# Attention: masked score tiles spread among the whole ones, where two followed each other at the end of a query tile

## What is computed

```python
q, k, v = split_heads(x @ Wq.T), split_heads(x @ Wk.T), split_heads(x @ Wv.T)
sim = einsum('bhid,bhjd->bhij', q, k) / sqrt(hd)
sim = where(causal_mask, neg, sim)
exp_sim = exp(sim - max(sim, axis=-1))
denom = sum(exp_sim, axis=-1) + exp(denom_bias)      # attention a; b has no bias
out = einsum('bhij,bhjd->bhid', exp_sim / denom, v)
```

## Time and profile before

| | us |
|---|---|
| median of 3 runs | 5185.71 (5184.31 to 5189.25) |
| the profiled execution | 5181.14 |
| its span | 5179.4 |
| PE busy | 4608.4 (89%) |
| DVE busy | 4098.5 (79%) |
| ACT busy | 3144.7 (61%) |
| POOL busy | 1188.4 (23%) |

### The profile page before, as it was taken

The page is one execution under the profiler, slowest core; times in us unless marked ns, Lnnn a source line. Parts: engine busy times, 40 slices in busy tenths (PEclk is TensorE's granted clock), DMA queues, the critical chain, the costliest instruction groups (busy, mean ns, idle before and its releaser), DMA issues. The chain is left out here.

```text
span 5179.4 us, 97856 instructions
## 1 busy us (share of the span) xinstructions
PE 4608.4 (89%) x40558; PEld 2002.5 (39%) x40558; DVE 4098.5 (79%) x4682; ACT 3144.7 (61%) x5855; POOL 1188.4 (23%) x1174
## 2 busy tenths in 40 slices
PE   5589999999997999689867899999999979996998
PEld 2322223322234555355533222232222345552555
DVE  5399999999875778477745999999998768774776
ACT  1267898889995334234323789888899933332433
POOL 0000001100003567243300000011000126662342
PEclk9699999999998999799977999999999989997999
DMA  3100000000000000400021000000000000005000
GB/s 125 47 20 8 2 14 14 14 14 2 2 2 21 1 1 1 147 1 0 1 68 34 17 8 2 19 9 14 14 2 2 2 19 1 1 1 147 9 12 13
DMA packets 70480, 106.94 MB, mean 21 GB/s; under 512 B 9465, under 2 KB 57721, under 8 KB 65919
## 3 DMA queue, kind: packets, MB, share of 16 engines
q1 hardware_dynamic: 70064, 101.08, 6.1%
HBM read 76.73 MB, written 23.08 MB: 19 GB/s over the span
## 5 line engine op out<-in xcount | busy, mean ns | idle before, releaser
L871 DVE TENSOR_REDUCE b_att_mx<-ps 128x2 f32<-128x1024 f32 (+3 forms) x1152 | 1227.3, 1130 | 112.4 <-PE ps L724 71.6
L871 DVE TENSOR_REDUCE a_att_mx<-ps 128x2 f32<-128x1024 f32 (+3 forms) x1152 | 1227.3, 1130 | 110.7 <-PE ps L724 69.7
L828 ACT ACTIVATE a_att_pt<-ps 128x512 f32<-128x512 f32 (+3 forms) x2304 | 1149.5, 561 | 212.7 <-PE ps L760 180.6
L828 ACT ACTIVATE b_att_pt<-ps 128x512 f32<-128x512 f32 (+3 forms) x2304 | 1149.7, 561 | 211.3 <-PE ps L760 179.6
L779 PE MATMUL ps<-b_att_pt,b_v 128*17 128x256 f32 (+1 forms) x8704 | 671.3, 381 | 9.7 <-ACT b_att_osb L815 9.0
L779 PE MATMUL ps<-a_att_pt,a_v 128*17 128x256 f32 (+1 forms) x8704 | 671.2, 381 | 9.7 <-ACT a_att_osb L815 9.1
L760 PE MATMUL ps<-b_q,b_k 51*128 51x512 f16 (+3 forms) x1152 | 367.0, 369 | 0.3 <-ACT b_att_pt L828 0.2
L760 PE MATMUL ps<-a_q,a_k 51*128 51x512 f16 (+3 forms) x1152 | 366.9, 369 | 0.3 <-ACT a_att_pt L828 0.2
L760 PE MATMUL ps<-a_att_q,a_att_k 51*128 51x512 f16 (+3 forms) x1152 | 340.4, 365 | 1.0 <-ACT a_att_pt L828 0.7
L760 PE MATMUL ps<-b_att_q,b_att_k 51*128 51x512 f16 (+3 forms) x1152 | 339.9, 365 | 1.3 <-ACT b_att_pt L828 0.5
L705 POOL TENSOR_SCALAR_AFFINE_SELECT b_att_pt<-b_att_pt 128x512 f32<-128x512 f32 x128 | 81.4, 636 | 1126.8 <-ACT b_att_pt L828 1114.4
(11 more groups left out here) (309 smaller groups left out, 7652.5 us busy)
## 6 DMA issues: line engine op xcount, KB each, us to landing
f_exp_w<-in_expert_w SPq DMA_DIRECT2D x64, 256.0 KB, 5.8
g_exp_w<-in_expert_w SPq DMA_DIRECT2D x64, 256.0 KB, 5.4
x<-in_x SPq DMA_DIRECT2D x1, 4096.0 KB, 19.6
a_parts_q<-a_qkv_cut SPq DMA_DIRECT2D x16, 256.0 KB, 2.8
a_parts_k<-a_qkv_cut SPq DMA_DIRECT2D x16, 256.0 KB, 2.7
b_parts_q<-b_qkv_cut SPq DMA_DIRECT2D x16, 256.0 KB, 2.8
b_parts_k<-b_qkv_cut SPq DMA_DIRECT2D x16, 256.0 KB, 2.7
out<-x SPq DMA_DIRECT2D x8, 512.0 KB
```

Of the source, the lines that this page charges most:

```text
L828: act.activation(pt[:, s % PT_RING, i, 0:width], ps[:, at:at + width], ACT.Exp, scale=unscale).then_inc(pt_ready, 1)
L871: dve.tensor_reduce(mx[u % 2][:, h:h + 2, t, c], both, AX.X, ALU.max).then_inc(ring_read, 1)
```

## The change

score_items gives the same tiles in another order. The whole tiles of a unit are listed in the old order (`whole`), the eight masked ones by pair and then by query tile (`ends`: t = 0, 1, 2, 3 of the first pair of heads, then of the second). Then the list is put together in eight blocks: about half of g whole pairs, one masked pair, the rest of the g whole pairs. For g = 0 only the eight masked pairs are left, in the order of `ends`. The wait for the loading of a quad's q and k (L720) is tied to the first item of the unit instead of to t = 0, c = 0 and head 1.

```diff
 def score_items(u):
 
     g = UNITS[u][1]
-    return [("S", u, 2 * pair + h, t, c, min(BANK, P * (KB * g + t + 1) - BANK * c))
-            for t in range(KB) for c in range(g + 1) for pair in range(2) for h in (1, 0)]
+    whole = [(pair, t, c, BANK) for t in range(KB) for c in range(g) for pair in range(2)]
+    ends = [(pair, t, g, P * (t + 1)) for pair in range(2) for t in range(KB)]
+    order = [item for j, end in enumerate(ends) for item in (*whole[j * g:j * g + (g + 1) // 2], end, *whole[j * g + (g + 1) // 2:(j + 1) * g])]
+    return [("S", u, 2 * pair + h, t, c, width) for pair, t, c, width in order for h in (1, 0)]
...
                 if h % 2 == 1:
                     wait(pe, ring_read, n - PAIRS + 1)
-                    if t == 0 and c == 0 and h == 1 and u % G == 0:
+                    if what == score_items(u)[0] and u % G == 0:
                         wait(pe, p_loaded[quad % 2], LOADS * ((quad + 1) // 2))
```

## The result

The changed kernel takes 5168.37 us (median of 8 runs, 5165.64 to 5175.15), the kernel before 5185.78 (median of 8, 5178.08 to 5189.25). The ratio is 0.9967, with a 95% interval of 0.9957 to 0.9978: faster by 0.3%, 17.4 us by the medians, 11 to 22 by the interval. The profiled executions (spans 5179.4 and 5167.5) are 11.9 us apart.

What follows compares the result with a forecast made beforehand. VectorE and TensorE hold each other up in the middle, neither the bound all the time. Gains of 8.9 - 0.5 = 8.4 us a layer, 16.8 for two, gave 5164.3 profiled, 5168.9 as median, said as 5169; low end 5154, high end 5184.

Steps and rivals of the forecast that it cites:

- the middle: Units 3 to 24 of each attention layer, 1,012 us, both engines near full; gain forecast 8.9 us a layer.
- the walk: Unit-by-unit count over the schedule with prices from the old trace; over units 3 to 24 it gave 8.9 us of 121.9.
- M: VectorE's copy of the maxima, 0.82 us; with a narrow pair right ahead 1.24 against 1.62 apart, another 0.4 gained.
- the two prices of a narrow pair: On VectorE, 0.82 us (0.87 for t = 2) with TensorE fully ahead, 1.09 with TensorE not ahead.
- a new wait at ScalarE: ScalarE, busy 857.46 of the 1,012 us, was expected to show no new wait; one would prove the walk wrong.
- The small units: Units with g = 1 lose (units 14 and 17: -0.35 and -0.6 us); g = 0 taken at nothing.
- Prelude and tail: Prelude, units 0 to 2: -0.5 us in unit 1; tail, units 25 to 31: nothing, VectorE having 59 us to spare.
- A: TensorE's advance regained only in part, mean pitch 0.90 for 0.856: 2.6 us a layer gained, 5180; chance 0.26.
- The sign named for it: For A: TensorE's waits as long as before; for the forecast: its wait ahead of M down from 10.5 us.
- B: Slower: TensorE falls behind at masked half-steps, now eight places a unit instead of four; 42 us more, 5228; chance 0.07.
- C: TensorE's clock falls in the middle, matmuls going at 1.2 GHz; tens of us lost; chance 0.01.
- D: Freed ring slot refilled in 0.7 us, not 0.8, where whole tiles follow without mask matmuls; 5150; chance 0.06.

Runs made afterwards that it cites:

- the cluster run: The changed kernel with all eight masked pairs of a unit together at its end: 5208.24 us, ratio 1.0048 to the kernel before.

## Why the prediction was right, and where it was not

The forecast was 5169.0, the median is 5168.4. The mechanism holds. The agreement to 0.6 us is luck: in undisturbed work the change brings 11.8 us, not the 16.8 of the sum, and the medians, 17.4 apart, have another 5.6 that no profile explains. The main term of the sum, the middle, was 8.9 a layer and came out at 4.8. By what VectorE did, from each start to the next, units 3 to 24 (us a layer):

| | before | after | change | the walk |
|---|---|---|---|---|
| the 132 narrow pairs | 122.1 | 113.5 | -8.6 | -8.9, with M |
| M | 18.4 | 19.7 | +1.3 | |
| the pairs 1,024 wide, and the reductions over key blocks | 853.5 | 855.3 | +1.8 | 0 |
| T and the divisions | 17.0 | 17.7 | +0.7 | 0 |

The narrow pairs themselves gave what was forecast. What the walk had too small or at nothing follows.

*What bounds the kernel, and the two prices of a narrow pair.* Right. With lead a lone narrow pair goes at 0.82 (0.86 for t = 2), without it at 1.03 to 1.09; the cluster run makes most of the later five pay the beat, and the time rises as worked out (15.2 us a layer over all 32 units, where 15 stood in the expectation; the medians have 25 for both).

*M, mis-sized.* The walk let a narrow pair right ahead of M save 0.4, by the nearest case in the trace before, 0.34 + 0.90. That narrow pair was the second of a couple, not a lone one. Behind a whole pair it is this (unit 7 of the changed kernel):

```profile
469.86 4.94 DVE L873 TENSOR_REDUCE a_att_mx<-ps 128x2 f32<-128x1024 f32 x5
474.80 0.22 DVE L868 COPY a_att_mt<-ps 48x128 f16<-48x128 f16 x1
475.93 9.81 DVE L873 TENSOR_REDUCE a_att_mx<-ps 128x2 f32<-128x1024 f32 x9 [0.91 <-PE ps L726]
```

Four whole pairs of the row of 5 end at 469.86 + 4 x 1.132 = 474.39, where the narrow one begins. It and M take 475.93 - 474.39 = 1.54, not 1.24; apart they would be 1.64. The copy is done at once, but the next pair comes one beat of TensorE later. Five units by 0.3 are 1.5 us a layer. Units 7, 9, 10, 21 and 22 together brought 1.8 us where the walk had 3.9.

*A wait that was left out.* In units 7 and 9 one whole pair behind a narrow one cost 1.41 and 1.50 in place of 1.13. On TensorE in unit 9 one sees what it stood behind:

```profile
628.17 0.63 PE L781 MATMUL ps<-a_att_pt,a_v 128*17 128x256 f32 x8 [0.33 <-ACT a_att_osb L817]
```

and on VectorE, right after:

```profile
629.41 2.36 DVE L873 TENSOR_REDUCE a_att_mx<-ps 128x2 f32<-128x1024 f32 x2 [0.28 <-PE ps L726]
```

The first product of a unit waits for ScalarE's copy of the last unit's result. The kernel before hid this behind VectorE's whole pairs in most units; where a narrow pair stands there, it is bare. The page of the kernel before had it, 9.1 us of idle time before layer a's products, and I put no price on it:

```profile
L779 PE MATMUL ps<-a_att_pt,a_v 128*17 128x256 f32 (+1 forms) x8704 | 671.2, 381 | 9.7 <-ACT a_att_osb L815 9.1
```

Units 7 and 9 brought -0.4 and -0.2 where the walk had a gain of 0.25 and 0.6. The prediction had called a new wait at ScalarE a sign against the walk; this one is old, and new only in that VectorE feels it.

*The small units.* Taken at -0.95 for units 14 and 17 and nothing for 15 and 16; measured, units 14 to 17 lose 1.3 (54.4 to 55.7), of which unit 16, with g = 0, loses 0.7, and the g = 2 units 13 and 18 lose 0.3 and 0.4 where 0.4 and 0.2 of gain stood. Two things meet here. The couples of these units were cheap already (a mean of 0.87 to 0.89 us a narrow pair before, 0.92 to 0.97 with g of 3 and more), and with one whole pair in a block or none the spread ones cost more (0.91 and 0.98; with two, 0.88). Keeping the couples there gives it all back.

*Prelude and tail.* Unit 1 lost 0.48 us (-0.5 predicted). One reading behind it was wrong: the 0.34 of the earlier trace rows is the step from a narrow pair to M's copy, not to the next pair; the second of the unit's other couples costs 0.61 and 0.87. The tail was taken at nothing, since TensorE is its bound on average; it gained 1.5 us a layer (322.0 to 320.5), and 0.3 to 0.6 in each of units 25, 27 and 28. The average over a stretch of 300 us hid that VectorE goes at its own pace for some pairs in a row, until a half-step without a score pair lets it catch up. Unit 25 of the kernel before, three whole pairs, a gap, and six more:

```profile
1287.03 3.49 DVE L871 TENSOR_REDUCE a_att_mx<-ps 128x2 f32<-128x1024 f32 x3 [0.62 <-PE ps L724]
1291.24 6.12 DVE L871 TENSOR_REDUCE a_att_mx<-ps 128x2 f32<-128x1024 f32 x6 [0.72 <-PE ps L724]
```

*The rivals.* A (the lead regained in part) was half true: undisturbed work alone would give 5174.0, between it and the forecast. The sign named for it came too. TensorE's waits at the ring, 21.7 and 10.5 us before, are these in the changed kernel:

```profile
PE ps L726 <- DVE a_att_mx L873: 27.5, 79, 0.8
...
PE ps L751 <- DVE a_att_mx L873: 7.0, 14, 0.7
```

Ahead of M they fell as forecast, in all they rose from 32.2 to 34.5. B (slower) did not come: lone narrow pairs go at 0.82, and without masks the advantage of spreading in the undisturbed units shrinks. Its premise is true in part: a masked half-step costs TensorE up to 0.12 us more, as the cluster run shows. C (the clock) was not a cost of the change: dips of the clock took a few us from either kernel's profiled run, none of the tens of us that C meant. By the rule on stops at the PSUM ring in "TensorE: Matmul & The Clock Gate" of the Trainium skill (A second HAM failure mode: psum-queue depth-cycling) such dips could be expected. The trace agrees in part: the dip shown above came behind a stretch in which TensorE had stopped for 1.25 of 6 us, but most stops at the ring brought none. D (the slot refilled faster than 0.8) did not show: 0.82 behind whole pairs. A third slot, which would answer the rule of "Perfetto Trace Analysis" of the Trainium skill (Optimization Strategy) on a gap that repeats, was not tried: four banks of the ring, three of the probability tiles and one of the result are all eight.

## What to carry to other kernels

Where two engines pass tiles through a shallow ring at nearly the same rate, a short tile is worth its saving only if the other engine is ahead when it comes; two short ones in a row, or one right beside an item that uses a ring slot for little work, pay the partner's full beat. Count what stands between them in the partner's spare time, not in tiles: a shortened step of the partner restores the lead at once, one long tile here a third of it. Price what stands next to the short tile too: here the narrow pairs gave all that was forecast, and nearly half of it was lost again at M and at the whole pairs beside them. And when a change is worth 0.2%, read it from units of work that repeat in the trace (here most to 0.01 us), outside dips of the clock, because the run's total moves by as much on its own.

## What the runs showed of the hardware

In the middle and the tail the granted clock stood at the upper of its two levels but for dips of 3 to 14 us to the lower one. Each of the ten profiled executions has one in unit 3 or unit 20, whose g is 3 and 4; elsewhere they came in unit 4 of one run, 7 of another, and 6 and 7 of a third. The smaller units 13 to 18 had none. Two of them cost 1.3 us (unit 3 of the changed kernel, 3.4 us long) and 3.4 us (its unit 20, 10.2 us long). In the kernel with couples and without the mask matmuls the stretch from 269 to 305 us had a granted clock of 0.85, against 0.98 with them, and unit 3 took 39.86 us in place of 37.19 in spite of less work. In the spread kernel the same stretch had 0.93 without the mask matmuls and 0.95 with them. So less work on TensorE can come with more dips, but didn't in both kernels. Why the dips come there and not at each stop is open.

VectorE's reductions overlap: one of 1,024 columns lasts 1.218 us, yet they follow each other at 1.132 us. So a sum of durations is too long by 0.086 us for each.
